# One load moved behind the fourth unit in SP's queue, and the last but one batch's rows shared four and four at the end

## The reference

```
masks = (adj == r) for r = 1..4             # 8 x 1024 x 1024 each
y     = sum_r masks_r @ x @ weight_r + bias
out   = layernorm(x + y), over the 128 features, eps 1e-5
```

## Time and profile before

| What | Value |
|---|---|
| Median of 3 runs | 109.86 us (109.48 to 110.02) |
| The profiled execution's own time | 109.88 us |
| Its span | 108.1 us, so 1.78 us lie around it |
| Instructions | 3122 |
| PE / PEld / DVE / ACT / POOL busy | 91% / 85% / 79% / 79% / 65% of the span |
| Moved by DMA | 42.23 MB, 391 GB/s over the span |

### The profile page before, as it was taken

One profiled execution on the slowest core, in us unless ns is written; L12 is line 12 of the kernel. 1 busy time (PEld: TensorE's weight loads), 2 busy tenths in 40 slices (PEclk: granted clock), 3 DMA queues, 4 the chain that ended last, 5 costly groups with the idle time before them and its releaser, 6 DMA issues.

```text
span 108.1 us, 3122 instructions
## 1 busy us (share of the span) xinstructions
PE 98.2 (91%) x1142; PEld 91.5 (85%) x1142; DVE 85.1 (79%) x254; ACT 85.0 (79%) x104; POOL 70.3 (65%) x134
## 2 busy tenths in 40 slices
PE   5937999999998999999999999999999999999700
PEld 5925999998897989998999899989999999999600
DVE  1024769456999999999998899689979699998960
ACT  0442787999996999699969996999697999867870
POOL 3000399796039989998999799979238604955650
PEclk9999999999999999999999999999999999999997
DMA  3999999999999999999999999999999999999136
GB/s 47 346 415 418 417 418 434 430 421 418 421 437 427 418 418 421 433 430 417 417 427 433 415 421 427 430 430 427 409 427 424 430 421 426 406 415 374 73 141 256
DMA packets 7794, 42.23 MB, mean 391 GB/s; under 512 B 865, under 2 KB 994, under 8 KB 4194
## 3 DMA queue, kind: packets, MB, share of 16 engines
q1 hardware_dynamic: 7344, 40.44, 90.3%
q10 hardware_dynamic: 434, 1.57, 3.7%
HBM read 37.81 MB, written 4.19 MB: 389 GB/s over the span
## 4 chain that ended last, share of the span: by engine, by line
PE 74%; DVE 11%; DMA 8%; ACT 2%; issue 1%; SPq 1%; DVEq 0%
PE h_ps L687 33%; PE ids_t L665 12%; PE y_ps L700 9%; PE h_ps L741 8%; DMA adj_sb<-adj 8%; PE ids_t L656 3%; DVE mask_t L868 3%; DVE row_max L843 2%; DVE x_sb L878 2%; ACT x_sb L583 2%; PE y_ps L741 2%; DVE stats L884 2%; PE spare L720 1%; PE h_ps L720 1%; PE other L720 1%
## 5 line engine op out<-in xcount | busy, mean ns | idle before, releaser
L548 ACT ACTIVATE bytes_of<-adj_sb,offset 128x2048 fp8e4<-128x2048 int32 x32 | 64.1, 2003 | 5.9 <-DMA adj_sb<-adj 5.4
L868 DVE TENSOR_SCALAR mask_t<-ids_t 128x1024 uint16<-128x1024 uint16 x62 | 40.0, 680 | 12.1 <-PE ids_t L656 10.9
L687 PE MATMUL h_ps<-mask_t,x_hi 128*128 128x256 bf16 (+1 forms) x200 | 25.1, 269 | 0.8 <-DVE mask_t L868 0.8
L687 PE MATMUL h_ps<-mask_t,x_lo 128*128 128x256 bf16 (+1 forms) x200 | 25.3, 269 | 0.2 <-DVE x_lo L939 0.2
L513 POOL TENSOR_SCALAR x_sb<-x_sb,rstd,shift 128x128 f32<-128x128 f32 x53 | 22.9, 448 | 0.9
L466 POOL TENSOR_TENSOR x_sb<-x_sb,bias_sb 128x1024 f32<-128x1024 f32 x6 | 14.3, 2375 | 11.1 <-ACT bias_sb L609 10.7
L687 PEld LDWEIGHTS h_ps<-mask_t,x_lo 128*128 128x128 f16 x200 | 18.9, 98 | 2.5 <-DVE x_lo L939 0.4
L687 PEld LDWEIGHTS h_ps<-mask_t,x_hi 128*128 128x128 f16 x200 | 18.0, 98 | 2.9 <-DVE mask_t L868 1.3
L665 PE MATMUL ids_t<-ident,bytes_of 128*128 128x128 bf16 x224 | 18.9, 227 | 0.0
L665 PEld LDWEIGHTS ids_t<-ident,bytes_of 128*128 128x128 bf16 x224 | 16.9, 148 | 1.4 <-ACT bytes_of L548 0.8
L884 DVE BATCH_NORM_STATS2 stats<-x_sb 128x6 f32<-128x128 f32 x62 | 13.5, 279 | 0.0
(11 more groups left out here) (102 smaller groups left out, 108.4 us busy)
## 6 DMA issues: line engine op xcount, KB each, us to landing
adj_sb<-adj SPq DMA_DIRECT2D x28, 1024.0 KB, 24.4
adj_sb<-adj SPq DMA_DIRECT2D x8, 512.0 KB, 10.4
out<-x_sb SPq DMA_DIRECT2D x7, 512.0 KB, 21.2
x_sb<-x SPq DMA_DIRECT2D x5, 512.0 KB, 23.7
x_sb<-x ACTq DMA_DIRECT2D x3, 512.0 KB, 7.7
out<-x_sb SPq DMA_DIRECT2D x2, 256.0 KB, 2.6
w_sb<-weight SPq DMA_DIRECT2D x1, 64.0 KB, 6.5
bias_row<-bias ACTq DMA_DIRECT2D x1, 0.5 KB
```

The source lines that it names most:

```text
L548: nc.scalar.activation(bytes_of[:, at % ROOM].rearrange("p n t -> p t n"), adj_sb[:, slot, 2 * k:2 * k + 2, :], ACT.Square, scale=SLOPE, b ...
L687: last = nc.tensor.matmul(h_ps[g.bank][:, to], part[:, g.b % 2, j, :], mask_t[:, g.b % 2, j, cols], start=(j == 0 and part is x_hi), stop= ...
L868: nc.vector.tensor_scalar(mask_t[:, b % 2, :, u * P:(u + 1) * P].bitcast(UINT16), ids_t[bank_of(turn)][:, :, :].bitcast(UINT16), 1 << bit, ...
```

## The change

It does three things. x of batch 6 is taken out of ACT's queue and issued by SP, behind unit 3 of batch 0. At the end, POOL normalises units 0 to 3 of batch 6 (before: 0 and 1) and ACT units 4 to 7 in one go (before: 4 to 7, then the root of rb, then 2 and 3), and ACT's first signal to SP comes behind units 4 to 7. On DVE, `offer_guess(ra)` stands ahead of `statistics(c)` and `combine(rb, c, ...)` instead of behind them.

```diff
             for u in range(1, J):
                 load_unit(0, u)
+                if u == 3:
+
+                    load_x(B - 2)
             load_x(1)
...
             roots(full)
-            normalise(full, full.units[:2])
+            normalise(full, full.units[:4])
             roots(ra)
...
             act.dma_start(bias_row[:, :], bias.rearrange("(a d) -> a d", a=1)).then_inc(s_bias, 16)
-            act.dma_start(units_of(x_sb[:, B - 2], B - 2, 0, J), rows_of(x, B - 2, 0, J)).then_inc(s_x[B - 2], 16)
             act.preload_act_table(ACT.Sqrt)
...
             root(ra)
-            normalise(full, full.units[4:])
+            normalise(full, full.units[4:]).then_inc(s_aside, 1)
             root(rb)
-            normalise(full, full.units[2:4]).then_inc(s_aside, 1)
             normalise(ra, ra.units[2:]).then_inc(s_aside, 1)
...
             find_wrong()
+            offer_guess(ra)
             statistics(c)
             combine(rb, c, c.units)
-            offer_guess(ra)
             statistics_of_sum(e)
```

## The result

The changed kernel takes 109.23 us (median of 10 runs, 108.88 to 109.43) against 109.81 us for the kernel before (10 runs, 109.48 to 110.02), a ratio of 0.9949 with a 95% interval of 0.9937 to 0.9962. That is 0.58 us or 0.5% less: small, but the whole interval lies under 1. The forecast was 109.4. All medians and ratios are of executions in the fast state, without two strays (559.5 us of guess_alone, 257.13 of the kernel before), except that three of the four of x6_behind_unit_5 are slow ones. The profiled execution took 109.19 us with a span of 107.4, against 109.88 and 108.1.

What follows compares the result with a forecast made beforehand. Landings of adj pairs were taken to set PE's instant at 71.75 us, and rb's store, behind full's and ra's, the end. Load 0, guess 0, four and four -0.49 from 109.88 gave 109.39, called 109.4 us; range 108.95 to 110.05.

Steps and rivals of the forecast that it cites:

- Bound of the kernel: Up to 71.75 us: landings of certain adj pairs set PE's instant, PE on time with them within some 0.05 us.
- the head's lead: At the start: unit 1's transposes up to 0.44 us sooner, with nothing left of it after 49.59 and 71.75.
- the waits near 49.6, 60.6 and 71.7: Sign of being right: PEld waits longer for ACT's checks at these instants; no size given.
- The load: At the start, x of batch 6 moved from ACT's queue to SP: worth 0, from bounds 0 and 0.44 us.
- x of batch 6 in time: At the start: it lands at about 13.2 us, ahead of PE's want at 14.05, a margin of 0.85 us.
- Rival C: At half 2, x of batch 6 lands late, each landing t costing t - 14.49; 110.9 us at 16.0; chance 0.13.
- Four and four: At the end, POOL and ACT share full's rows, full's store goes at 102.31 instead of 103.67: -0.49 us.
- The guess: On DVE at the end, ra's guess offered earlier: taken as 0, rb's root delayed by 0 to 0.14 us, hidden.
- The sum: Whole kernel: load 0, guess 0, sharing of rows -0.49, so 109.88 - 0.49 = 109.39 us, called 109.4.
- Rival A: At the end, rb's store still lands 2.7 us behind its issue, so no gain: 109.9 us; chance 0.15.
- Rival B: At the start, pairs land earlier too and up to 0.44 us passes through to the end: 108.95 us; chance 0.12.

Runs made afterwards that it cites:

- guess_alone: The kernel before with only the guess for ra offered ahead of statistics(c) on DVE: 109.72 us, ratio 0.9993 to the kernel before.
- x6_behind_unit_5: The changed kernel with x of batch 6 loaded two units later, behind unit 5 instead of unit 3: median 112.20 us of four runs.
- end_alone: The kernel before with only the edits at the end (rows four and four, guess offered earlier): 109.28 us, ratio 0.9956 to the kernel before.
- load_alone: The kernel before with only the load of x of batch 6 moved from ACT's queue to SP: 109.77 us, ratio 0.9999 to the kernel before.

## Why the prediction was right, step by step

- **Bound of the kernel.** The tie of PE with the landings was read rightly: +512 KB cost 1.22 us, -512 KB gave 1.0 to 1.3. What the prediction had in part wrong is the place. It let the head's lead die at 49.59 and 71.75; it dies at 24.87 and 27.35 already. So one of its signs failed: the waits near 49.6, 60.6 and 71.7 were to grow, and are 0.25, 0.25 and 0.33 us where they were 0.24, 0.27 and 0.31. In the profile before, the first two ties don't show as waits of PEld, as PE came to them within 0.05 us of the end of the check. In the other traces with the load in ACT's queue, where unit 0 came sooner, they do show (in end_alone 0.17 us at 24.92 and 0.29 at 27.39).
- **The load: 0 from 0 to 0.44.** Measured 0.9999. The upper bound was a little small: from unit 0's transposes to unit 1's PEld now takes 9.22 - 6.34 = 2.88 us, and in load_alone 9.51 - 6.62 = 2.89, against 9.82 - 6.44 = 3.38 in guess_alone (the load in place): a lead of 0.49. The rest of the 0.94 us is that unit 0 itself came at 6.34 in this execution and at 6.79 in the one of before; guess_alone, with the load in place, has 6.44, so that is scatter between executions.
- **x of batch 6 in time.** PE didn't wait for it at 13.55. By the view of its issue it landed at 12.65 (9.0 behind its issue at 3.65), where about 13.2 was forecast: a margin of 0.9 us against 0.85. Rival C didn't come about. Its price, every microsecond of lateness in full, was wrong in two ways by the runs of x6_behind_unit_5: it left out that PE has room ahead of the next ties (the 0.88 us of idle at 24.87 and what its own pace gives back; one of the four runs was only 1.13 us slower, where in the traced one the load landed 3.1 us after PE would have wanted it), and it left out the clock.
- **Four and four, 0.49.** end_alone gave 109.76 - 109.28 = 0.48. full's issue: forecast 102.31, measured 102.20 in a run in which all is 0.11 sooner from 71.6 on. POOL's roots of ra: 101.44, measured 101.34. product: 102.04, measured 101.82, as it followed 0.48 behind the start of the roots and not 0.60. That term was misread from the row: the idle of 0.60 us ended at 101.69, so POOL had been free from 101.09 on, 0.51 behind the start. The three rows: 103.51, measured 103.30. ACT's: 103.45, measured 103.22. rb's issue: 104.89, measured 104.67. With the 0.11 taken off, each lies within 0.12 us.
- **The guess: nothing.** 0.9993 alone, and 109.30 against 109.28 in the company of the sharing.
- **The sum.** 109.39 against 109.23. The forecast counted from the profiled execution's 109.88; as a difference it is 0.49 against 0.58. The missing 0.09 would fit rb's issue, which came 0.11 sooner than forecast for that step of POOL (the same in end_alone). But end_alone, with the same step, gave 0.48 us, so the times don't resolve it.
- **Rival A** fell with the landing after 2.2 us and the two kernels without full's store. The Trainium skill's fit ("DMA: Bandwidth & Descriptors", "Anatomy of one DMA", 2.0 us plus bytes over 436 GB/s, for GpSimd's path) would, as an estimate, have given that rival its 2.6 us for 256 KB. These stores, issued by SP, took 2.0 us for 256 KB when nothing lay ahead and 2.6 for 512 KB, so the measurement decides: less the 0.63 and 1.26 us of their bytes, a fixed part near 1.4 us.
- **Rival B** fell with load_alone: 109.77 us, and the transposes at 71.71.

## What to carry to other kernels

Where two resources both look full, one long stretch of the chain can't tell which sets the pace: look whether the engine's start at the next hand-over is free or tied, and give a dose of 512 KB more to see the slack in one run. Work saved ahead of a tie is lost at the first tie, which need not be one that the profile shows as a wait. At the end of this kernel a store landed behind the bytes queued ahead of it (2.7 us behind its issue with 768 KB in the stream ahead, 2.0 alone), so give SP the large store early, and then balance the engines so that the last two stores don't follow each other closer than their bytes take.

## What the runs showed that was not expected

In the one traced execution with x of batch 6 late, an idle time of 2.69 us of PE near the start was followed by about 3 us at half the granted clock (0.50 at 18 to 19 us, 1.00 again from 21). By the estimate above that about doubled what the late transfer cost; the one of four runs that came out at 110.36 us paid 1.13 us in place of some 3. And a sharing of three and five rows gave another 0.45 to 0.56 us, nearly as much as the whole change, from one row moved.
